# A 16-head graph attention layer on one core: value tables split head by head inside the main loop, adjacency products gathered into rounds behind 14 heads, adjacency turned in byte pairs, and the correction of the sums done by group on GpSimd

## What is computed

```python
seq = (x @ W_seq).reshape(N, H, DH)
score1 = einsum('nhd,d->hn', seq, a1); score2 = einsum('nhd,d->hn', seq, a2)
scores = leaky_relu(score1[:, :, None] + score2[:, None, :], 0.2)
scores = scores + (1.0 - adj)[None, :, :] * -65500.0
attn = softmax(scores, axis=-1)
hidden = einsum('hij,jhd->ihd', attn, seq).reshape(N, D)
out = layernorm(x + elu(hidden @ W_out + b_out))      # x is (2048, 512), adj is (2048, 2048) of 0 and 1
```

## Time and profile before

| what | value |
|---|---|
| median of 3 executions | 595.35 us |
| the profiled execution | 595.52 us |
| its span in the profile | 593.7 us |
| granted TensorE clock, mean | 0.974 |
| stage 1 | 0 to about 95 us |
| preparation and split stage | about 95 to 149 us |
| heads 0 to 12, with adjacency products | about 149 to 442 us |
| heads 13 to 15 | about 442 to 506 us |
| tail | 506 to 594 us |

### The profile page before, as it was taken

How to read it: one execution, slowest core, us unless ns; L and a number is a source line. 1 busy time by engine, 2 the same in 40 slices (tenths; PEclk the granted TensorE clock), 3 DMA queues, 4 the chain that set the end, 5 groups by cost and what they waited for, 6 DMA issues and landing times.

```text
span 593.7 us, 17557 instructions
## 1 busy us (share of the span) xinstructions
PE 522.0 (88%) x6931; PEld 461.9 (78%) x6931; DVE 526.1 (89%) x793; ACT 418.7 (71%) x442; POOL 60.7 (10%) x77
## 2 busy tenths in 40 slices
PE   3999995167999999999999999999998777799981
PEld 2788884167999999999999999999997767444440
DVE  4777777999979999999999999999999999789996
ACT  2666665446988988889889889889889986322220
POOL 4000001343000000000000000000000000434432
PEclk9999999599999999999999999999999999799997
DMA  7777742000111020120120110220210220123333
GB/s 260 280 262 264 261 160 77 3 3 10 64 73 52 24 73 22 54 73 10 65 73 2 73 73 2 73 72 2 73 73 2 72 73 1 53 72 124 106 121 109
DMA packets 13656, 49.53 MB, mean 83 GB/s; under 512 B 1680, under 2 KB 2704, under 8 KB 9488
## 3 DMA queue, kind: packets, MB, share of 16 engines
q1 hardware_dynamic: 13600, 48.67, 23.2%
HBM read 44.34 MB, written 4.33 MB: 82 GB/s over the span
## 4 chain that ended last, share of the span: by engine, by line
PE 61%; DVE 20%; issue 11%; ACT 3%; DVEq 1%; POOL 1%; DMA 1%; ACTq 0%; SPq 0%; POOLq 0%
PE bank L342 30%; PE bank L322 16%; PE bank L278 9%; DVE tring L640 3%; ACT wide L465 3%; PE bank L288 2%; DVE tring L652 2%; DVE Vp L607 2%; PE bank L378 2%; DVE Vp L695 2%; DVE Vp L705 2%; DVE Vp L687 1%; DVE Vp L701 1%; DVE xpb L601 1%; PE bank L269 1%
## 5 line engine op out<-in xcount | busy, mean ns | idle before, releaser
L342 PE MATMUL bank<-Vp,tring 128*128 128x132 f16 x4096 | 278.3, 221 | 14.0 <-DVE tring L652 9.4
L475 ACT ACTIVATE tring<-abc,ab 128x2048 int8 (+1 forms) x144 | 281.8, 2024 | 0.0
L342 PEld LDWEIGHTS bank<-Vp,tring 128*128 128x128 fp8e4 x4096 | 244.3, 98 | 23.1 <-DVE tring L652 17.2
L652 DVE TENSOR_TENSOR tring<-adjT,tring 128x512 uint32<-128x512 uint32 x256 | 168.4, 684 | 17.7 <-ACT tring L475 17.6
L322 PE MATMUL bank<-Vp,adjT 128*128 128x132 f16 x2048 | 157.5, 222 | 25.1 <-DVE Vp L607 17.2
L322 PEld LDWEIGHTS bank<-Vp,adjT 128*128 128x128 fp8e4 x2048 | 130.2, 97 | 26.1 <-issue 17.3
L640 DVE TENSOR_SCALAR tring<-abc,ab 128x2048 int8 (+1 forms) x112 | 143.3, 1280 | 0.0
L278 PE MATMUL bank<-Vp,abc 128*128 128x272 f32 x256 | 64.1, 404 | 0.6 <-DVE Vp L523 0.6
L378 PE MATMUL bank<-abc,Vp 128*128 128x512 f32 x128 | 59.7, 611 | 3.7 <-ACT Vp L498 3.7
L278 PEld LDWEIGHTS bank<-Vp,abc 128*128 128x128 f32 x256 | 48.6, 196 | 11.0 <-DVE Vp L523 1.8
L465 ACT ACTIVATE wide<-bank 128x396 f32<-128x396 f32 x96 | 35.9, 480 | 29.0 <-PE bank L342 20.7
(11 more groups left out here) (73 smaller groups left out, 343.6 us busy)
## 6 DMA issues: line engine op xcount, KB each, us to landing
tring<-in_adj_dram SPq DMA_DIRECT2D x16, 1024.0 KB, 4.9
abc<-a_rows SPq DMA_DIRECT2D x16, 1024.0 KB, 4.7
abc<-in_x_dram SPq DMA_DIRECT2D x16, 256.0 KB, 3.6
Vp<-in_x_dram SPq DMA_DIRECT2D x16, 256.0 KB, 2.7
out_dram<-Vp SPq DMA_DIRECT2D x16, 256.0 KB, 2.0
Vp<-in_L_gnn_W_seq_dram SPq DMA_DIRECT2D x4, 256.0 KB, 5.5
abc<-in_L_gnn_W_out_dram SPq DMA_DIRECT2D x1, 1024.0 KB, 5.1
Vp<-in_L_gnn_b_out_dram SPq DMA_DIRECT2D x1, 256.0 KB, 3.7
```

What stands on the lines that cost most here:

```text
L342: mm = pe.matmul(bank[b][:, c * 2 * VW:(c + 1) * 2 * VW], tslot[jt % RING][:, it * P:(it + 1) * P].bitcast(F8), Vp[:, h, jt, :, :], start= ...
L475: act.activation(tslot[jt % RING], row, ACT.Sign, bias=ab[:, jt, bass.ds(h + H, 1)], scale=-1.0).then_inc(u_ready, 1)
L652: dve.tensor_tensor(slot, adjT[:, jt, :].bitcast(U32), slot, ALU.bitwise_and).then_inc(t_ready, 1)
```

## The change

- **Values per head.** The separate split stage is gone. Head 0's table is split before the main loop; the others are split inside it, one or two a head (`SPLITS`), a few heads ahead of their use: GpSimd scales the values of both sets in one instruction of 128x1024 and two of 128x16 (`values`), ACT writes the high halves behind tile 13 (or 7), DVE the low halves behind tile 14 (or 8).
- **Rounds.** There are no early products. The 64 products stand in rounds of 4 to 6 behind heads 1 to 14 (`ROUNDS`), each product whole, after the head's 256 matmuls. The ring has 12 slots instead of 8. ACT copies the banks of the head before behind tile 5, and one adjacency sum behind each tile after it.
- **Byte pairs.** ACT casts adj to bytes (64, or 64 + 56 with an edge), six tiles of which share slots of the ring. TensorE turns pairs of bytes as f16: 8 transposes a tile. Node order is changed so that a pair is two nodes of neighbouring tiles (`x_n`, `out_n`, `adj_n`). The copy out of PSUM is one of 128x2048 bytes, on DVE for even tiles and on ACT for odd ones.
- **Combination.** DVE only joins high and low sums of a head (`join`, two instructions of 128x528, into `cab`). The subtraction, the multiplication and the addition are done for four heads at once on GpSimd (`finish`, three instructions of 128x2112), except for the last head, which DVE does.
- The counted loops are written out.

```diff
+ROUNDS = (0, 5, 5, 6, 4, 4, 4, 4, 4, 4, 4, 4, 5, 5, 6, 0)
+SPLITS = ((1, 2), (3,), (4,), (5, 6), (7,), (8,), (9,), (10,), (11,), (12,), (13,), (14,), (15,), (), (), ())
+BANKS_AT = 5
+SUMS_AT = 10
+HIGH_AT = ((13,), (7, 13))
+LOW_AT = ((14,), (8, 14))
-RING = 8
+RING = 12
```

Stage 1 on SP:

```diff
+            for t in range(NT):
+                r = t % 2
+                if t >= 2:
+                    sp.wait_ge(x_turned, t - 1)
+                    sp.dma_start(xs[:, r, :], x_t(t)).then_inc(x_loaded[r], 16)
+                    sp.wait_ge(adj_cast, t - 1)
+                sp.dma_start(stage[:, r, :], adj_n[t // 2, t % 2]).then_inc(adj_loaded[r], 16)
```

Stage 1 on ACT, and then on DVE:

```diff
+            copy_x(0)
+            for t in range(NT):
+                if t + 1 < NT:
+                    copy_x(t + 1)
+                cast_adj(t)
+                if t % 2 == 0 and t > 0:
+                    copy_adj(t - 1)
...
+            for t in range(NT):
+                fix_adj(t)
+                copy_seq(t)
+                if t % 2 == 1:
+                    copy_adj(t - 1)
```

The rounds on TensorE, behind the 256 matmuls of head h:

```diff
+                for s in round_range(h):
+                    it, g = s % NT, s // NT
+                    pe.wait_ge(v_ready, GRP * (g + 1))
+                    if s >= 2:
+                        pe.wait_ge(adj_copied, s - 1)
```

A head on DVE:

```diff
-                    for step in range(5):
-                        if not first and jt == FINISH_AT[step]:
-                            finish_head(h, step, adj_sums)
+                    if h > 0 and jt == SUMS_AT:
+                        join(h - 1)
+                    for k, at in zip(SPLITS[h], LOW_AT[len(SPLITS[h]) - 1]):
+                        if jt == at:
+                            split_low(k)
...
+            def join(h, tiles=slice(0, NT)):
+                dve.wait_ge(banks_copied, BANKS * h + -(-tiles.stop // ITB))
+                if h % GRP == 0 and h > 0:
+                    dve.wait_ge(grp_step, 3 * (h // GRP))
+                for s in range(2):
+                    part = slice(s * HW, (s + 1) * HW)
+                    sums = dve.scalar_tensor_tensor(out=cab[:, tiles, h % GRP, part], in0=raw[:, tiles, 1, part], scalar=1.0 / LO[s],
+                                                    in1=raw[:, tiles, 0, part], op0=ALU.mult, op1=ALU.add)
```

GpSimd:

```diff
+            def values(k):
+                pool.wait_ge(v_ready, k)
+                for s in range(2):
+                    pool.tensor_scalar(xp[:, :, s, DH], E[:, :, s, k], TOP * LO[s], None, ALU.mult)
+                pool.tensor_tensor(xp[:, :, :, 0:DH], seq[:, :, k * DH:(k + 1) * DH].unsqueeze(2).to_broadcast([P, NT, 2, DH]),
+                                   Es[:, :, :, k:k + 1].to_broadcast([P, NT, 2, DH]), ALU.mult).then_inc(xp_made, 1)
+            def finish(g, heads):
+                n, first = heads, GRP * g
+                sums = acc[:, :, HW * first:HW * (first + n)].rearrange("p t (h c) -> p t h c", c=HW)
+                pool.wait_ge(adj_copied, NT * (g + 1))
+                pool.wait_ge(joined, first + n)
+                pool.tensor_tensor(sums, sums, cab[:, :, 0:n, HW:VW], ALU.subtract).then_inc(grp_step, 1)
...
+            for k in range(1, 9):
+                values(k)
+            pool.wait_ge(r_out, 1)
+            finish(0, GRP)
+            for k in range(9, 13):
+                values(k)
+            finish(1, GRP)
+            for k in range(13, H):
+                values(k)
+            finish(2, GRP)
+            finish(3, GRP - 1)
```

More of the change, by code:

```diff
@@ L108, in gat_kernel @@
+        misc = early[:, NT * H:]
         mx, diag, ones, mcol = misc[:, 0:32], misc[:, 32:64], misc[:, 64:64 + P], misc[:, 200:201]
         Mb = misc[:, 208:208 + 2 * H]
[L110 to L125, removed]
+        vinv = misc[:, 240:240 + H]
@@ L185, in gat_kernel @@
[L185 to L198, removed]
-            with eng.Fori(4 // slots, NT // slots) as k:
-                for q in range(slots):
-                    body(slots * k + q, q)
-            for i in (NT, NT + 1):
-                body(i, i % slots)
+        x_n = x.rearrange("(q p s) d -> q s p d", p=P, s=2)
@@ L313, in _ @@
+            pe.wait_ge(diag_ready, 1)
             pe.matmul(bank[5][:, 0:2 * H], ones[0:2 * H, :], diag[0:2 * H, :], start=True, stop=True).then_inc(mx_spread, 1)
-            for half in range(2):
-                pe.wait_ge(adj_ready[half], 1 + NT)
+            turn_adj(NT - 1)
             pe.wait_ge(a_copied, 4)
-            def adj_product(r, it, g, js):
-                for j in js:
-                    for s in range(2):
-                        mm = pe.matmul(bank[6 + r][:, 0:GRP * HW], adjT[:, j, it * P:(it + 1) * P].bitcast(F8),
-                                       Vp[:, GRP * g:GRP * (g + 1), j, s, HW:VW],
-                                       start=(j == 0 and s == 0), stop=(j == NT - 1 and s == 1))
-                if j == NT - 1:
-                    mm.then_inc(adj_done, 1)
@@ L471, in head @@
+            split_high(0)
+            for h in range(H):
+                row_loaded(act, h)
+                behind = list(round_range(h - 1)) if h > 0 else []
                 for jt in range(NT):
                     if jt not in DVE_TILES:
-                        act.wait_ge(t_free, NT * h + jt + 1)
-                        act.activation(tslot[jt % RING], row, ACT.Sign, bias=ab[:, jt, bass.ds(h + H, 1)],
+                        slot_free(act, h, jt)
+                        act.activation(slot(h, jt), row(h), ACT.Sign, bias=ab[:, jt, H + h:H + h + 1],
@@ L488, in _ @@
-            head(ADJ_HEADS, False, True, False)
-            with act.Fori(ADJ_HEADS + 1, H) as h:
-                head(h, False, False, False)
-            copy_sums(H)
-            def tail(i, r):
-                if live(i, 0):
+                    if h > 0 and jt == BANKS_AT:
+                        copy_banks(h - 1)
+                    if jt > BANKS_AT and behind:
+                        copy_adj_sums(behind.pop(0))
+                    for k, at in zip(SPLITS[h], HIGH_AT[len(SPLITS[h]) - 1]):
+                        if jt == at:
+                            split_high(k)
@@ L495, in tail @@
+            copy_banks(H - 1)
+            for i in range(NT + 1):
+                if i < NT:
                     act.wait_ge(h_turned, i + 1)
-                    if past(i, 2):
+                    if i >= 2:
                         act.wait_ge(z_made, i - 1)
-                    act.copy(hT[:, r, :], bank[r][:]).then_inc(h_copied, 1)
-                if live(i, 1):
+                    act.copy(hT[:, i % 2, :], bank[i % 2][:]).then_inc(h_copied, 1)
+                if i >= 1:
                     act.wait_ge(zmin_ready, i)
-                    act.activation(et[:, 1 - r, :], et[:, 1 - r, :], ACT.Exp).then_inc(e_ready, 1)
@@ L586, in _ @@
+            dve.wait_ge(e_scaled, 2)
             for s in range(2):
[L587 to L594 removed]
```

630 lines of the change are left out of this document (281 added, 349 removed).

## The result

| kernel | median of 4 | lowest to highest |
|---|---|---|
| before | 595.36 us | 594.75 to 596.28 |
| changed | 604.72 us | 603.66 to 607.46 |

The ratio is 1.0163 (95% interval 1.0127 to 1.0199): slower by 1.6%. The profiled execution of the changed kernel took 607.46 us, 2.7 more than the median, with a span of 605.2 us at a mean granted TensorE clock of 0.942 (before 0.974). Its spread maximum comes at 99.24 us, and at 97.4 to 98.2 in the five profiled kernels of the experiments that load x in the same order.

A forecast was written before the change was run, and what follows sets the result against it. TensorE bounds stage 1 and heads 0 to 12 before; after the change DVE, stopped by GpSimd, bounds heads 4 to 12. 595.5 + 9.7 (last head's end) - 2.5 (tail) = 602.7, say 603 us; range 576 to 614.

The forecast's parts named there:

- The sign: Whole kernel: slower than before, given 0.64; faster 0.31; within 0.2% of no change 0.05.
- by these numbers alone: Main loop without GpSimd's interference: DVE 20.5 us and TensorE 22.2 us per head, so a large gain.
- DVE's loss per GpSimd instruction: Main loop: GpSimd stops DVE 1.95 us per head for values, 3.9 per combination instruction, 11.6 per group.
- TensorE's round waits for the copy of the sum: Rounds: first sum copied 2.5 us behind the head's end, needed at 3.7, so no cost.
- the bank wait between heads goes: Between heads: banks are copied while TensorE does the round, so its wait for them disappears.
- Head 15: GpSimd's last group takes 9.5 us, to 512, inside head 15; if later, the tail waits for it.
- Stage 1: Before the loop: fewer transposes save 7.2 us, late x loads take back 5.6; spread maximum at 99.7 us.
- stage 1 keeps its 7.2 us: Rival: x lands 3.5 us after issue, nothing is taken back, 597 us; no separate chance given.
- The tail: After the last head: same work without the loop, 0.4 us saved per pair of tiles, 2.5 in all.
- The loop: Main loop: last head ends at 515.6 us instead of 505.9, +9.7.
- GpSimd doesn't stop DVE: Rival, main loop: GpSimd's work fits DVE's gaps or runs in parallel, 563 us; less stop, 563 to 590, chance 0.25.
- longer instructions or no turn: Rival: GpSimd's instructions exceed 4.1 us or get no turn, and join waits; 605 to 620 us, chance 0.15.

The follow-up runs named there:

- the two kernels with idle work: Kernel before plus nine GpSimd instructions of 128x2048 on an unused buffer, at ends of heads 4, 8, 12: subtractions 619.93 us, memsets 596.17 us.

## Why the prediction came out as it did

**The sign and the mechanism** were right. GpSimd's work in the loop stops DVE, heads with a combination become DVE's, and the gain of the rearrangement is lost to it. Without GpSimd in the loop the same rearrangement takes 573.9 us, and 569.3 with x loaded earlier: the large gain "by these numbers alone" was there. The size, 603 against 604.7, was partly luck. The profiled execution is 3.3 us behind the forecast at head 3, 7.6 at head 4, only 4.0 at head 12, because heads 5 to 12 took 207.6 us and not 211.3, and 6.6 at the end, of which the tail gives 2.3 back. Term by term:

- **DVE's loss per GpSimd instruction, forecast 3.9 us and 1.95 us for the values.** Measured from the means of DVE's instructions: values 1.5 per head (above); the 12 instructions of the combination 256 x (0.814 - 0.705) + 112 x (1.561 - 1.431) = 42.5 us, 3.5 each. Both a little smaller. With 1.5, DVE's head is 22.0 and no longer above TensorE's 22.2. This is why heads 6 to 8, 10 and 11 come every 22.3 us, by TensorE, where 22.5, by DVE, was forecast: outside the heads with a combination DVE did not become the bound.
- **TensorE's round waits for the copy of the sum, "no cost".** This step failed. Of head 4's 30.4 us, 26.0 were forecast. In the double split of head 3, GpSimd's two small instructions, of 16 numbers each, waited for their turns (7.22 below), its values came late, and ACT, whose queue holds the high half ahead of its comparisons, copied the banks late (head 3 had ended at 207.4):

```profile
119.91 5.98 POOL L643 TENSOR_SCALAR xp<-E 128x16 f32<-128x16 f32 x2 [9.01 <-DVE Vp L528]
...
131.53 0.51 POOL L643 TENSOR_SCALAR xp<-E 128x16 f32<-128x16 f32 x2 [2.69 <-DVE Vp L528]
131.97 1.96 POOL L644 TENSOR_TENSOR xp<-acc,Es 128x1024 f32<-128x1024 f32 x1
...
190.56 7.22 POOL L643 TENSOR_SCALAR xp<-E 128x16 f32<-128x16 f32 x2 [6.02 <-DVE Vp L528]
196.60 4.13 POOL L644 TENSOR_TENSOR xp<-acc,Es 128x1024 f32<-128x1024 f32 x1
```

```profile
211.34 2.20 ACT L405 ACTIVATE raw<-bank 128x396 f32<-128x396 f32 x6
213.41 0.30 ACT L411 ACTIVATE acc<-bank 128x132 f32<-128x132 f32 x1
```

```profile
213.85 9.31 PE L321 MATMUL bank<-Vp,adj 128*128 128x132 f16 x128 [2.54 <-ACT acc L411]
```

  The forecast charged only what GpSimd takes from DVE, and not what DVE takes from GpSimd: 0.51 us for the two small ones where DVE was idle (131.53), 5.98 and 7.22 where it was not. Those who wait for GpSimd pay it. It was in heads 0, 1, 3 and 4; from there on the values are needed so late that it costs nothing. Between heads 0 and 1, where no round covers the copy of the banks, TensorE waited 3.59 for it; "the bank wait between heads goes" did not hold there. The two kernels with the values on DVE, whose head 1 ends at 153.1 and head 4 at 227.6 without the combination (155.3 and 234.5 with the values on GpSimd), show the size.
- **TensorE's clock** was no term of the sum. Behind the wait of 2.54 in head 4 it was granted 0.59 and then 1.00, and 0.50 in the last 11 us of head 12, with a wait of 6.46 in it (columns as above):

```profile
213.85:218.00 4.15, 4.15 (x44) 4.15 (x45) 3.90 (x5) 2.81 (x4) 0.00 (x0) 0.59 0.00 0
434.00:446.00 12.00, 6.17 (x54) 5.73 (x55) 12.00 (x9) 1.78 (x5) 7.09 (x2) 0.50 0.11 38
```

  What it costs can be read in head 4, because the kernel without the combination has the same wait with 1.00 behind it:

```profile
212.01 7.90 PE L321 MATMUL bank<-Vp,adj 128*128 128x132 f16 x128 [2.53 <-ACT acc L411]
```

  The same 128 matmuls take 7.90 there and 9.31 here, and head 4 takes 28.9 us and not 30.4. So of the 4.4 us that head 4 took too long, 2.5 are the wait and 1.4 the clock.
- **Head 15.** The last group's work was placed inside it without a price. It runs there, from 506.4 to 517.0; a comparison takes 3.89 and two ands 6.93 beside it, and the head is about 2.0 us longer (round of head 14 at 494.3, end 522.3, against 11.2 + 14.8 = 26.0 for TensorE alone).
- **Stage 1.** Spread maximum forecast for 99.7, first comparison of head 0 for 107.4:

```profile
91.86 0.17 DVE L459 TENSOR_SCALAR Vp<-Vp 128x4 int8<-128x4 f32 x1 [2.67 <-ACT tring L363]
...
99.24 0.19 DVE L497 COPY raw<-bank 128x32 f32<-128x32 f32 x1 [0.78 <-PE bank L292]
...
106.57 1.28 DVE L552 TENSOR_SCALAR tring<-abc,ab 128x2048 int8<-128x2048 f32 x1
```

  At 99.24 and 106.57, with the late fixing of the last tile (91.86, a wait of 2.67 for its cast) as forecast. That is this execution; the five others with the same order of loads, at 97.4 to 98.2, were 1.5 to 2.3 us ahead of the forecast. Loads of x land 5.6 us after their issue (page, median; before 3.6), as the prediction took. Its term, about 1 us at each of five tiles and 5.6 in all, came out as the four waits of 4.4 us, and loading x earlier gave 3.8 back: right in kind, a little too large. The rival "stage 1 keeps its 7.2 us" is excluded by it.
- **The tail,** forecast -2.5, is 605.2 - 521.67 = 83.5 against 593.7 - 505.34 = 88.4: -4.8. The saving per pair of tiles was 0.75 us and not 0.4: two tiles take 8.48 now, and 9.23 before. What gives the other 0.35 was not followed.

```profile
566.52 0.66 DVE L596 TENSOR_TENSOR Vp<-bank,Vp 128x512 f32<-128x512 f32 x1
...
575.00 0.66 DVE L596 TENSOR_TENSOR Vp<-bank,Vp 128x512 f32<-128x512 f32 x1
```

The loop came out at +16.3 instead of +9.7 in the profiled execution, the tail 2.3 better, and that execution itself lies 2.7 above the median. The rival "GpSimd doesn't stop DVE" is excluded by the two kernels with idle work. Of "longer instructions or no turn" the first half did not hold as priced (means 4.4, 4.6 and 5.5 us, with the wait for the turn in them, while DVE lost 3.5), the second did, though at the values and not at the join.

What stays open: byte pairs and the 12-slot ring were not undone alone. That the rearrangement with GpSimd idle in the loop is worth 22 us (573.9), and 26 with x ahead and the last copy first (569.3), is measured; how it divides is not.

## What to carry to other kernels

Before moving work from DVE to an idle GpSimd, price it on DVE: here the values took 1.3 us on DVE and 1.5 from it when GpSimd did them, an instruction of 2112 numbers 2.35 on DVE and 3.5 from it, and in the kernel's time the combination cost 11.4 us on DVE and 31.9 on GpSimd. An idle engine that shares a resource with the bound one isn't free. Charge the exchange in both directions: what the moved work takes from the busy engine, and how late it comes because it waits for it, with everything queued behind whoever needs it. And a change of several parts can hold a gain that its one bad part hides: undo the parts one at a time.

## What the runs showed of the hardware

- GpSimd's smallest instructions are hurt most: two of 128x16 take 0.51 us together beside an idle DVE and 1.8 to 7.2 beside a busy one, mostly 4.2.
- GpSimd's reading stops DVE, its writing does not: 40.3 us of subtractions cost 24.4 us; 21.9 us of memsets cost 0.7, within the noise (ratio 0.9998 to 1.0023).
- A load of 256 KB issued 0.4 us behind one of 1 MB on the same queue lands 5.6 us after its issue (median), instead of 3.6 where it was issued 2.0 us behind.
- Behind the waits of 2.5 to 6.5 us shown above, TensorE was granted 0.50 to 0.62 for the next stretch, its lower level of 1.2 GHz for all or most of it; in another run, behind a wait of 2.53, it was granted 1.00 throughout. The same 128 matmuls took 9.31 us and 7.90.
